# Weighing the values of a second attention layer: value slices in four column groups in fp32, in place of exponentials and values split into bf16 halves

## What is computed

```python
def _L1_xattn_ref(x, cond, w_q, w_k, w_v, w_out, b_out):
    N_HEADS = 16
    D_HEAD = 64
    ...
    scale = D_HEAD ** (-0.5)
    q = (x @ w_q).reshape(B, SQ, N_HEADS, D_HEAD)
    k = (cond @ w_k).reshape(B, SKV, N_HEADS, D_HEAD)
    v = (cond @ w_v).reshape(B, SKV, N_HEADS, D_HEAD)
    attn = jnp.einsum('bqhd,bkhd->bhqk', q, k) * scale
    attn = jax.nn.softmax(attn, axis=-1)
    out = jnp.einsum('bhqk,bkhd->bqhd', attn, v).reshape(B, SQ, N_HEADS * D_HEAD)
    return out @ w_out + b_out
```

## Time and profile before

| | |
|---|---|
| time, median of three runs | 958.36 us (952.79, 958.36, 963.0) |
| span of the profiled execution, first to last instruction | 894.0 us |
| granted PE clock, mean over the span | 0.979 |
| PE busy | 836.1 us |
| DVE busy | 577.2 us |
| ACT busy | 537.0 us |
| POOL busy | 450.6 us |
| second attention, first to last exponential | 316.8 to 741.3 us |

### The profile page before, as it was taken

The page is one execution under the profiler, slowest core; times in us unless marked ns, Lnnn a source line. Parts: engine busy times, 40 slices in busy tenths (PEclk is TensorE's granted clock), DMA queues, the critical chain, the costliest instruction groups (busy, mean ns, idle before and its releaser), DMA issues.

```text
span 894.0 us, 30924 instructions
## 1 busy us (share of the span) xinstructions
PE 836.1 (94%) x12318; PEld 711.1 (80%) x12318; DVE 577.2 (65%) x1613; ACT 537.0 (60%) x1132; POOL 450.6 (50%) x544
## 2 busy tenths in 40 slices
PE   6999999788899989999999999999999998899994
PEld 3566666543899869999999999999999997797994
DVE  5788888842124367777777777777777675644662
ACT  3788888541566656666666656657667653225772
POOL 7123444466013136556556566575574443673664
PEclk7899999999999999999999999999999999999997
DMA  5333432211665235641010010110110000345440
GB/s 155 111 111 109 130 118 81 80 34 52 188 193 152 78 103 159 195 145 32 18 32 26 23 33 20 29 32 20 30 32 11 21 3 1 98 146 160 129 123 8
DMA packets 75215, 71.98 MB, mean 81 GB/s; under 512 B 13409, under 2 KB 66984, under 8 KB 74306
## 3 DMA queue, kind: packets, MB, share of 16 engines
q1 hardware_dynamic: 67138, 55.05, 21.0%
q0 software_dynamic: 7136, 14.71, 5.2%
q10 hardware_dynamic: 800, 0.24, 0.1%
HBM read 37.72 MB, written 30.49 MB: 76 GB/s over the span
## 4 chain that ended last, share of the span: by engine, by line
PE 76%; DVE 8%; issue 7%; POOL 4%; ACT 2%; DMA 2%; SPq 0%; POOLq 0%; DVEq 0%; ACTq 0%
PE of L1124 8%; PE sf L1088 8%; PE jf L1018 6%; PE sf L1073 5%; PE mf L1053 5%; PE sf L1299 4%; PE sf L1289 4%; PE jf L1027 4%; PE sf L1027 3%; PE sf L1210 3%; PE sf L1330 2%; PE sf L851 2%; POOL out L796 2%; PE mf L1111 2%; PE of L897 2%
## 5 line engine op out<-in xcount | busy, mean ns | idle before, releaser
L720 POOL TENSOR_TENSOR pl<-pT,ph 128x512 bf16<-128x512 f32 x128 | 146.0, 1164 | 132.4 <-DVE ph L1784 131.9
L1790 DVE TENSOR_REDUCE cmxb<-mf 128x8 bf16<-128x1024 f32 x64 | 78.3, 1224 | 57.4 <-PE mf L1111 57.4
L664 POOL DMA_INDIRECT buf<-gu,slots x64 | 63.7, 995 | 64.8 <-PE of L897 46.2
L1632 DVE TENSOR_REDUCE cmx<-mf 128x8 bf16<-128x1024 f32 x64 | 78.3, 1224 | 24.2 <-PE mf L878 23.7
L1476 ACT ACTIVATE pT<-sf 128x1024 f32<-128x1024 f32 x64 | 66.9, 1045 | 25.1 <-PE sf L1094 25.1
L1088 PE MATMUL sf<-qTs,kTs 64*128 64x128 f32 x1024 | 74.4, 285 | 0.1
L709 POOL DMA_INDIRECT gb<-eo,slots x56 | 57.6, 1029 | 26.3 <-DMA eo<-rows 13.4
L1394 ACT ACTIVATE pTf<-sf 128x1024 f32<-128x1024 f32 x64 | 62.5, 1019 | 10.0 <-PE sf L858 9.7
L1088 PEld LDWEIGHTS sf<-qTs,kTs 64*128 64x128 f32 x1024 | 62.2, 187 | 5.8 <-issue 0.3
L1457 ACT CAST kTb<-mf 128x512 bf16<-128x512 f32 x30 | 17.6, 585 | 81.2 <-PE sf L1053 81.2
L2045 DVE TENSOR_TENSOR rows<-sf,dn 128x256 f32<-128x256 f32 x40 | 17.0, 425 | 72.2 <-PE sf L1299 71.8
(11 more groups left out here) (284 smaller groups left out, 2609.3 us busy)
## 6 DMA issues: line engine op xcount, KB each, us to landing
buf<-zero SPq DMA_DIRECT2D x12, 516.0 KB, 7.4
ctxT<-in_ctxP SPq DMA_DIRECT2D x32, 192.0 KB, 2.8
rows<-buf SPq DMA_DIRECT2D x47, 129.0 KB, 2.1
buf<-zero SPq DMA_DIRECT2D x20, 256.0 KB, 3.5
rows<-buf SPq DMA_DIRECT2D x40, 128.0 KB, 2.3
eo<-rows SPq DMA_DIRECT2D x40, 128.0 KB, 2.3
gu<-in_gu SPq DMA_DIRECT2D x4, 1024.0 KB, 7.0
rows<-in_x SPq DMA_DIRECT2D x8, 256.0 KB, 5.1
```

Source lines behind the costliest of these rows:

```text
L664: nc.gpsimd.indirect_dma_start(out=buf0[:, :], out_offset=bass.IndirectOffsetOnAxis(ap=slots0[:, k, b:b + 1], axis=0), in_=xna0[:, b, :], ...
L720: nc.gpsimd.tensor_tensor(pl[h][:, :, c, :], pT[h][:, :, c, :], ph[h][:, :, c, :], ALU.subtract)\
L1632: nc.vector.reduce_max(to, mf[:, :, :].rearrange("p c (j k) -> p c j k", j=QH), AX.X)\
L1790: nc.vector.reduce_max(cmx1[b % 2][:, :].rearrange("p (r k) -> p r k", r=2)[:, :, 4 * h:4 * h + 4], M1p[:, :, :].rearrange("p r (c k) -> p ...
```

## The change

weigh() is turned over. The weights are now 32-column slices of the values (va1, fp32, without a column of ones), the exponentials pT (fp32) stream past them, and the output has features in the partitions and queries along the row: head j of a group writes to partitions 32j to 32j+31, slice u (of two) to columns 128u to 128u+127. A third product with 32 columns of ones (ones32) gives the sum of the exponentials in columns 256 to 383, repeated over 32 partitions. That is 12 fp32 products of 128x32 weights and 128 columns for a group, where there were 16 bf16 products of 128x128 weights and 65 columns.

evacuate() takes the reciprocal of 128x128 sums, where it took 128x4, and its multiplication writes oT directly. high_half, low_values, low_halves, the fills oT0 and oT1 and ACT's copies of them are gone. y waits for evacuate (pv_free). oT has two buffers. w_out's rows are put in the new order of the features on the host.

```diff
@@ PE @@
                     if name == "y":
-                        L1.free(pe, "oT0", n)
-                        L1.free(pe, "oT1", n)
+                        pe.wait_ge(L1.pv_free, 4 * n + 4)
...
-                    elif what == "oT":
-                        pe.wait_ge(L1.pv_free, 4 * n + 2 * h + 2)
-                        for c in range(4):
-                            last = nc.tensor.transpose(ps[:, c * P:(c + 1) * P],
-                                                       o1[p][:, 8 * h + 2 * c:8 * h + 2 * c + 2, :], ident[:, :])
...
                 def weigh(b, g):
 
                     p, h = b % 2, g // 2
-                    pe.wait_ge(L1.pl_done, 4 * b + g + 1)
+                    pe.wait_ge(L1.exp_done, 2 * b + h + 1)
                     pe.wait_ge(L1.v_free, 2 * b + 2 - h)
                     need(pe, L1.pv_free, 4 * b + g)
-                    for j in range(QH):
-                        n, r = 2 * (g % 2) + j // 2, j % 2
-                        for m, (pp, part) in enumerate(((ph, 0), (ph, 1), (pl, 0), (pl, 1))):
-                            last = nc.tensor.matmul(of[:, j * (D1 + 1):(j + 1) * (D1 + 1)], pp[h][:, r, n, :],
-                                                    va1[p][part][:, QH * g + j, :], start=(m == 0), stop=(m == 3))
+                    for u in range(3):
+                        for j in range(QH):
+                            n, r = 2 * (g % 2) + j // 2, j % 2
+                            w = ones32[:, :] if u == 2 else va1[p][:, QH * g + j, 32 * u:32 * u + 32]
+                            last = nc.tensor.matmul(of[32 * j:32 * j + 32, u * P:(u + 1) * P], w, pT[h][:, r, n, :],
+                                                    start=(u == 0), stop=(u == 2))
                     last.then_inc(L1.pv_full, 1)
...
@@ ACT @@
                 def exponential(b, h):
 
                     act.wait_ge(L1.s_full, 4 * b + 2 * h + 2)
                     if b >= 1:
-                        act.wait_ge(L1.pl_done, 4 * (b - 1) + 2 * h + 2)
+                        act.wait_ge(L1.pv_full, 4 * (b - 1) + 2 * h + 2)
...
@@ DVE @@
                 def evacuate(b, g):
 
                     dve.wait_ge(L1.pv_full, 4 * b + g + 1)
-                    ov = of[:, 0:QH * (D1 + 1)].rearrange("p (h d) -> p h d", d=D1 + 1)
-                    nc.vector.reciprocal(rden[:, :], ov[:, :, D1]).then_inc(L1.rden_done, 1)
+                    nc.vector.reciprocal(rden[:, :], of[:, 2 * P:3 * P]).then_inc(L1.rden_done, 1)
                     dve.wait_ge(L1.rden_done, 4 * b + g + 1)
-                    nc.vector.tensor_tensor(o1[b % 2][:, QH * g:QH * (g + 1), :], ov[:, :, 0:D1],
-                                            rden[:, :].unsqueeze(2).broadcast_to([P, QH, D1]), ALU.mult)\
+                    nc.vector.tensor_tensor(oT[b % 2][:, 2 * g:2 * g + 2, :],
+                                            of[:, 0:2 * P].rearrange("p (u n) -> p u n", u=2),
+                                            rden[:, :].unsqueeze(1).broadcast_to([P, 2, P]), ALU.mult)\
                         .then_inc(L1.pv_free, 1)
```

More of the change, by code:

```diff
@@ L138, in step_fills @@
     else:
-        order = [("q1", b + 1), ("q0", b + 2), ("oT0", b - 1), ("oT1", b - 1), ("y", b - 1)]
+        order = [("q1", b + 1), ("q0", b + 2), ("y", b - 1)]
     return [(name, n) for name, n in order if inside(n)]
@@ L145, in bank_for @@
     if b >= LAST:
-        return {"oT0": 0, "oT1": 2, "y": 0}[name]
+        return 0
     if (name, n) == ("q0", 2):
@@ L150, in bank_for @@
         return 1
-    return {"q0": 0, "q1": 2, "oT0": 1, "oT1": 2, "y": 2}[name]
+    return {"q0": 0, "q1": 2, "y": 2}[name]
 def moved_at(b):
@@ L272, in build @@
         veA, rsA, veF, rstd = [sb(n, [P, NB]) for n in ("veA", "rsA", "veF", "rstd")]
-        xrn = [sb(f"xrn{p}", [DM, P]) for p in range(2)]
         wq0 = sb("wq0", [DM, DM])
@@ L283, in build @@
         xnT = [sb(f"xnT{p}", [DM, P]) for p in range(2)]
-        ctxT = [sb(f"ctxT{p}", [P, CB, P]) for p in range(2)]
-        va1 = [[sb(f"va1{p}{n}", [P, NH, D1 + 1], BF16) for n in "hl"] for p in range(2)]
-        rden = sb("rden", [P, QH])
+        ones32 = sb("ones32", [P, 32])
+        rden = sb("rden", [P, P])
         with ExitStack() as front_only:
@@ L1066, in values_of @@
                         pe.wait_ge(L1.exp_done, 2 * n)
-                        L1.free(pe, "oT0", n - 2)
+                        pe.wait_ge(L1.k_free, 2 * n + 2)
                         if inside(n + 1):
@@ L1230, in drain @@
                     score_half(LAST, 1)
-                    fill("oT0", LAST - 1)
-                    fill("oT1", LAST - 1)
                     weigh(LAST, 0)
@@ L1242, in drain @@
                     shared_gate(2)
-                    fill("oT0", LAST)
-                    fill("oT1", LAST)
                     shared_down(1)
@@ L1522, in attention @@
                             take("q0", b + 2)
-                        take("oT0", b - 1)
                         exponential(b, 1)
-                        take("oT1", b - 1)
                         take_values(b + 1)
@@ L1542, in drain @@
                     nc.scalar.activation(table[:, :], mhalf[:, 0:1], ACT.Silu)
-                    take("oT0", LAST - 1)
-                    take("oT1", LAST - 1)
                     shared_gate(0)
@@ L1548, in drain @@
                     shared_gate(2)
-                    take("oT0", LAST)
-                    take("oT1", LAST)
                     shared_gate(3)
@@ L1918, in attention @@
                         evacuate(b, 0)
-                        high_half(b, 1)
                         if inside(b - 2):
                             normal_after(b - 2)
-                        low_values(b + 1)
                         evacuate(b, 1)
```

83 lines of the change are left out of this document (20 added, 63 removed).

## The result

The changed kernel takes **1004.02 us** (median of four, 1002.54 to 1005.85); the kernel before took 959.15 us beside it (median of four). The ratio is 1.0477, with a 95% interval of 1.0430 to 1.0523. That is slower, as forecast, and inside the range of 963 to 1005, but 20 us above the 984 that was named.

A forecast was written before the change was run, and what follows sets the result against it. PE, busy throughout the second attention's loop, was taken as the bound; +23.2 (29 batches at +0.80), +2 choose_expert, -1.3 start and +1.6 drain gave +25.5 us, so 958.4 became 984 us, range 963 to 1005.

The forecast's parts named there:

- third rival: Evacuation on DVE: the 128x128 reciprocal takes 1.2 us, batch +1.32 us, total 1000 us; chance 0.14.
- The reciprocal: Evacuation on DVE: 128 elements in a partition take 950 ns, where 176 stood, four times a batch.
- first rival: Evacuation on DVE: the reciprocal is short (0.31 us), no evacuation late, batch +0.54 us, total 972 us; chance 0.12.
- W: PE time from a new weigh's start to the next block: 0.81 us; four cost 3.24 us, where they cost 2.07.
- fourth rival: PE's weigh: column groups don't run side by side, a weigh takes 2.5 us, total about 1175 us; chance 0.01.
- the second (0.63): PE's weigh: changing form costs nothing and the reciprocal is short, batch -0.12 us, total 950 us; chance 0.06.
- The batch step by step: Second attention's batch on PE grows from 13.55 to 14.35 us: work 0.29, exponential 0.15, evacuations 0.36.
- The exponential's wait behind oT1: Before values_of: oT1 filled PE's wait for exponential(b, 1); without it PE stalls 0.15 us a batch.
- Start, drain, choose_expert: Outside the regular batch: start -1.3 us, drain +1.6 us, choose_expert's operations in DVE's queue +2 us.
- The step that failed: Whole launch: span goes from 894.0 to about 919.5 us, with the launch's median 64.4 us above it left unchanged.
- The assumption about POOL: POOL in the loop: no work on this path, removed subtractions count as nothing, gathers never late.
- the sentence on the clock: PE in the loop: granted clock assumed still at 1.00 because the gaps are short; a fall would mean more time.

The follow-up runs named there:

- short oT1: Kernel before with only one of oT1's four transposes left in batches 1 to 29; 958.88 us, ratio 0.9969.
- small reciprocal: Changed kernel with the reciprocal taken of 128x4 sums, not 128x128, and spread over columns; 910.26 us (1.0152) on the first chip, 977.17 us (1.0185) on the third.
- late gathers: Changed kernel with POOL's two gathers per batch moved behind evacuate(b, 0); 927.61 us (1.0330) on the first chip, 992.01 us (1.0351) on the third.

## Why the prediction was right, and where it was off

**The direction and the mechanism held.** PE had no idle time to give, and both things that the forecast counted came: more work on PE, and waits for an evacuation that had been hidden.

**That 1004.02 lies inside the range is in part luck.** Its top, 1005, came from the third rival, a reciprocal of 1.2 us (1000), and 5 us of spread, and the row of 954 ns rules that rival out. What brought the time there stood in no rival: signals of PE seen late, and one odd batch. The same kernel on the second chip, 56.3 us above the kernel before beside it, would have lain outside.

**The reciprocal**: 954 ns, forecast 950. The third rival (1.2 us) and the first (0.31) fall with it. The Trainium skill (VectorE: DVE Perf Modes, First, the fixed hardware budget) led to an estimate of 1.2 us; the row decides, 954 ns.

**W**: 0.80 (537.75 to 538.55), forecast 0.81. The fourth rival (2.5 us for a weigh) and the second (0.63) fall.

**The batch step by step**, from 536.12: weigh(b-1, 2) at 1.63 (forecast 1.64); reciprocal 2.98 (2.89); weigh(b-1, 3) 4.53 (4.45); scores 5.33 (5.26); weigh(b, 0) 7.11 (6.90); values_of 7.90 (7.86); weigh(b, 1) 9.67 (9.61); turn 10.46 (10.42). The evacuations' stalls came at the three places named. The one for weigh(b, 0) is 0.2 later than forecast, since weigh starts 0.08 later and DVE takes its reciprocal up 1.02 after weigh's start (541.67 against 540.65), not 0.89; and it covers the wait for the exponential, which ends at 7.80 (forecast 7.73): of the 0.15 forecast for it nothing shows as its own. This batch takes 14.54 with its choose_expert. Whole: 14.31 where no signal is late and choose_expert is absent, forecast 14.35. That is **+0.76 and not +0.80**.

**The exponential's wait behind oT1** is shown by the short oT1: no gain from three quarters of the transposes gone.

**The small reciprocal**, which is the first rival made real, has a batch of 14.03, worked out as 14.09.

**Start, drain, choose_expert.** In the trace with late gathers choose_expert makes a batch 0.23 longer than its neighbours where it made it 0.13 longer before. That holds for five of its six batches in the loop (the forecast counted seven); in the sixth, behind the last gather, it is 0.13 as before. So it is **0.5 and not 2**. At the start PE's wait of 2.53 became 0.96 for ACT's copy, -1.6, and shorter waits for ACT and for the first evacuations came in its place: the first three periods grew by 1.2 us together, where three others grow by 2.3. That is -1.1, forecast -1.3. From batch 30's first exponential to batch 31's, where the drain begins, it was 10.57 and is 12.11, +1.5, and from there to the last product of y it was 17.1 and is 18.0: together +2.5, forecast +1.6 for the whole drain.

**The batch that nobody forecast.** In every trace of the changed kernel with the whole reciprocal one early batch is 17.8 to 20.6 us long. The late-gathers kernel on the first chip, PE, and then the stretch behind it, with the granted clock as the last figure but two:

```profile
381.06 0.39 PE L1097 MATMUL of<-pT,ones 128*32 128x128 f32 x5
383.77 0.41 PE L1097 MATMUL of<-pT,ones 128*32 128x128 f32 x3 [2.32 <-issue]
...
383.50:388.50 5.00, 4.73 (x45) 4.07 (x44) 1.92 (x5) 2.01 (x4) 0.00 (x0) 0.66 0.03 9
```

PE stops for 2.3 us in the middle of a weigh, between two instructions that wait for no semaphore, and the clock that was at 1.00 falls to 0.66 on the mean of the next 5 us, which means 1.2 GHz for the larger part of them. Together this is 4.3 us (18.59 against 14.31). The stop comes at the same place (three or four of the ones' products are left) in all seven of these traces and takes 2.3 to 2.6 us, and here DMA's share from 380.50 to 383.50 is 0.82. The two traces with the small reciprocal and those of the kernel before have no such batch. That PE's instructions came late behind those transfers would fit; no run tried it, and the cause stays open.

**The step that failed: "The span goes from 894.0 to about 919.5", and the launch's 64.4 us "which I leave as it is".** The difference of +25.5 was taken from a quick chip's trace and added to another kind's time. On the quick chip it is about right: the changed kernel with late gathers costs 29.0 there (927.6 less 898.6), which is the forecast's 25.5, the odd batch's 4.3 and 0.8 less. That the parts come so close is in part chance, for the single ones were off by 0.2 to 1.5 us, in both directions. The changed kernel itself didn't run on that chip, so that its own number there stays open; the small reciprocal, with the gathers unmoved, met no late signal there. On the other kind the loop has some 19 us on top. From batch 1's first exponential to batch 30's the changed kernel needs 441.1 us in its trace on record, and the kernel before 394.5 on the third chip, +46.6; on the first chip the same stretch grew by 27.1 (420.2 against 393.1). So 46.6 less 27.1, **19.5 us, is put down to late signals** in a kernel whose evacuation has no slack. This sets a kernel with late gathers on the one chip against one with early gathers on the other, so that it also holds what the place of the gathers costs on the first chip; for the kernel before that was nothing. Kernels with traces on both chips show the effect without that mixture: over the same stretch the third chip takes 1.4 us more than the first with the kernel before, 8.6 with the small reciprocal (415.8 against 407.2), and 12.4 with late gathers (432.6 against 420.2, of which 2.0 lie in the odd batch). The whole difference of the spans is 47.6 (1001.2 less 953.6).

**The assumption about POOL** ("POOL has no work on this path ... the gathers behind them on POOL's queue are never late") was true of the gathers' own time and missed what they do to others. And the sentence on the clock (1.00 through the loop) held but for the odd batch.

What isn't settled: why a chip is of one kind or the other (only one of the quick kind was met in the experiments), whether the signal itself comes late or its reader, and how much of the 58 us outside the second attention comes from it. There the rows above are single examples, and the clock has a part that no run took apart: from 100 to 200 us and from 200 to 300 the granted clock was 0.93 and 0.88 on the third chip, 0.98 and 0.97 on the first. It is shown that late signals come with the same kernel on one chip and not on another, that they go with POOL's indirect transfers (batches after the last gather are 14.31 everywhere), and that they move with them (14.70 and no wait of 1.23 when they stand later).

## What to carry to other kernels

An evacuation in one PSUM bank between two uses has a slack; work it out from the timeline before the evacuation is made longer, as here 3.1 us of DVE's time a batch cost little on DVE and 0.28 us on PE (14.31 against 14.03), and the rest came from the weighing and from a wait that other work had filled. Count a reciprocal's elements in a partition before a product is turned over: with the queries in the partitions there were 4 sums in each (178 ns), with the queries along the row there are 128 (954 ns). And a trace shown beside run times need not come from the same chip: compare its span with them first, for a gap of 64 us was here a second chip, on which slack that looks ample may be none.

## What the runs showed of the hardware

- The kernel before takes 898.6 us on one chip and 959 to 962 on others. Of the 60 us between two of its traces 1.5 lie in the second attention, whose loop PE bounds, and 58 outside it.
- On the slower chips DVE and ACT start up to 1.8 us after PE's results are complete when POOL issues indirect transfers around that time, 0.04 to 0.12 on the other. In the rows shown the late start lies 0.33 to 1.26 us behind the end of one of POOL's instructions, so it isn't tied to it closely. For the batch this costs 0.4 to 1.3 us in the changed kernel and at most 0.16 in the kernel before.
- A stop of 2.3 us on PE and the clock's fall after it (0.66 on the mean of 5 us) cost 4.3 us in one batch.
- DVE's reciprocal takes 178, 249, 353 and 954 ns for 4, 16, 32 and 128 fp32 elements in a partition, 6.3 ns an element from 4 to 128.
